# A two-layer transformer on one core: the same instructions in another planned order, from a plan that prices the tensor engine's changes of array mode and the delays between engines differently

## The chip, the core and the metric

The kernel runs on one core of a Trainium2 chip. Its engines work side by side, each through its own list of instructions: TensorE (PE, with its weight loads as PEld), VectorE (DVE), ScalarE (ACT), GpSimd (POOL), and SyncE (SP), which issues the transfers. They wait for each other by semaphores only. The metric is the time of one execution on the device, in microseconds (us).

## The reference, cut to what matters

Eight sequences of 1024 tokens of width 256 go through two layers, all in float32. Each layer is attention and then a feed-forward part, each added to its input:

```
x = x + attn0(layernorm(x))      # 16 heads of 16, causal, softmax
x = x + ffn0(layernorm(x))       # gates by entmax15 over 16 experts, GELU
x = x + attn1(layernorm(x))      # 16 heads of 16 from a latent of 64, half of each head rotated by position
x = x + ffn1(layernorm(x))       # shared squared-ReLU block; routed experts count only where a gate is exactly 1
```

## The kernel before, in words

A sequence is cut in two halves of 512 queries (`c` is 0 or 1). A pass is one half of one layer of one sequence; the half with `c` = 1 sees 1024 keys, the other 512. A pass has four units, each of four heads (`u`, 0 to 127). What one unit does:

- `ld`: its stacks of K and Q (float16 pieces of the float32 numbers) are loaded from DRAM, four transfers on SP.
- `s` (line 1282, masks on line 1296): TensorE makes scores by query, two banks at a time, and VectorE takes the largest of each row (lines 1877, with the causal mask, and 1880).
- `mx`, `mt`: GpSimd splits the maxima, TensorE turns them (line 1307), ScalarE copies them (line 1625), two transfers put them beside Q.
- `st` (line 1321): TensorE makes the scores again, transposed and with the maximum taken off, two banks at a time; ScalarE takes the exponential (line 1616), GpSimd clears what lies above the diagonal (line 1777).
- `pv` (line 1340): TensorE weighs the values; ScalarE copies the sum out (`o`, line 1631), and transfers and a division follow (`os`, `ol`, `rc`, `rs`, `rl`, `dv`).

Beside the units run the chains of the other work: layer norms (`rstd`, `norm`, `xt`), projections (`qk_`, `qk`, line 1251, `v_`, `v`, line 1259), the output product (`ao_`, `ao`), the feed-forward parts (`lg` to `fo`, with the GELU products `hid` on line 1395 and `z` on line 1400; `rt` to `down`). Every result of TensorE takes one of seven banks of the accumulation memory, which comes free when VectorE or ScalarE has read it.

What sets the order: before the kernel is built, `program_order()` (from line 603) plays the run through in a small model, `Plan`, and writes down one list, ORDER. Each engine then walks this list and issues its own part of it, so the model fixes the order on all engines and which bank each product takes; on the chip only semaphores decide when something starts. In the model a product takes its entry of TIMES (or a formula), a change of the array's mode costs SWITCH (`run`, from line 304; MODES says which products use the whole array, `full`, and which only 64 rows, `rows`, or strips of 32 columns, `strips`), a result is seen by the next engine SEEN later, and where several things could be next, that with the lowest rank is taken. The ranks are a row of RULES, one for each window of the program (27 windows, each with up to two passes and the chains that run beside them): `s` and `st` for a score step, `fed` and `fed_st` for the same while the engine that reads them has more than `feed_dve` or `feed_act` us of work, `pair` for two `pv` in a row, `due` and `chain` for the other products, `stay` the penalty for leaving the array's mode.

The line of `projection` that the change edits orders the first steps too: wmax is the largest weight by which the first layer's Q and K weights are scaled, `wm`, `sca` (line 1233), `scb` (line 1238).

## Time and profile before

| | |
|---|---|
| median of 3 runs | 2695.77 us (2695.38 to 2698.12) |
| the profiled execution | 2700.38 us, its span 2698.4 us |
| granted TensorE clock, mean over the span | 0.964 of 2.4 GHz |
| busy PE, DVE, ACT, POOL | 2440.8, 2042.8, 1869.6, 1031.5 us |
| instructions | 53735 |

The span is the time from the first to the last instruction of the program. TensorE is busy for 90% of it, but a matmul counts as busy while it waits inside the array too, so this is no proof that the array works at its peak.

### The profile page before, as it was taken

How to read it: one execution, taken by the hardware profiler on the slowest of the kernel's cores; microseconds unless marked ns; L12 is line 12 of the kernel's file. 1: busy time of each engine (PE TensorE's matmuls, PEld its weight loads, DVE VectorE, ACT ScalarE, POOL GpSimd, SP SyncE). 2: the span in 40 equal slices, each digit the busy share in tenths (PEclk: the TensorE clock that was granted, in tenths of full speed). 3: DMA queues.
4: the chain of work that ended last, by engine and by line, in shares of the span. 5: the costliest groups of instructions: out<-in, count | busy, mean ns of one | idle time of the engine just before them, and what ended most of it. 6: DMA issues, size and time to landing. Idle time of an engine off the chain costs nothing. (4 is left out here: it accounts for less than half of the span.)

```text
span 2698.4 us, 53735 instructions
## 1 busy us (share of the span) xinstructions
PE 2440.8 (90%) x17565; PEld 976.1 (36%) x17565; DVE 2042.8 (76%) x5616; ACT 1869.6 (69%) x3804; POOL 1031.5 (38%) x1710
## 2 busy tenths in 40 slices
PE   6889789999899998999999999999999999989785
PEld 3324233334333343333433343333433334334223
DVE  4884787967879578885888779786897868784862
ACT  3577467777677766687677777677677777856572
POOL 2324443254424363153532545244452534343221
PEclk9899899999899999999999999999999999989897
DMA  5311222224212242222421133212331222211211
GB/s 189 93 46 48 88 68 87 69 74 120 93 60 81 65 124 81 64 74 73 121 82 60 64 100 116 66 61 75 117 107 55 86 84 86 76 57 45 78 56 65
DMA packets 192482, 219.47 MB, mean 81 GB/s; under 512 B 36912, under 2 KB 143824, under 8 KB 192208
## 3 DMA queue, kind: packets, MB, share of 16 engines
q1 hardware_dynamic: 192208, 215.97, 26.1%
q8 instruction: 153, 2.51, 0.4%
q14 instruction: 121, 0.99, 0.1%
HBM read 113.07 MB, written 101.71 MB: 80 GB/s over the span
## 5 line engine op out<-in xcount | busy, mean ns | idle before, releaser
L1616 ACT ACTIVATE probs<-ps 128x512 f32<-128x512 f32 (+2 forms) x2560 | 1245.7, 560 | 465.8 <-PE ps L1321 458.6
L1880 DVE TENSOR_REDUCE mx<-ps 128x1 f32<-128x512 f32 (+2 forms) x1536 | 897.4, 638 | 233.4 <-PE ps L1282 134.0
L1877 DVE CUSTOM_DVE_ANT_0 ps<-ps,mask_b 128x512 f32<-128x512 f32 (+1 forms) x1024 | 613.7, 651 | 188.3 <-PE ps L1282 179.2
L1777 POOL TENSOR_SCALAR_AFFINE_SELECT probs<-probs 128x256 f32<-128x256 f32 (+1 forms) x768 | 368.9, 484 | 930.9 <-ACT probs L1616 927.1
L1340 PE MATMUL ps<-probs,vaug 128*17 128x512 f32 (+3 forms) x6144 | 602.3, 501 | 14.8 <-ACT probs L1616 6.1
L1282 PE MATMUL ps<-stk_k,stk_q 48*128 48x512 f16 (+3 forms) x3072 | 460.9, 336 | 87.5 <-issue 29.0
L1321 PE MATMUL ps<-stk_q,stk_k 50*128 50x512 f16 (+3 forms) x3072 | 451.5, 333 | 70.2 <-DVE mx L1877 23.1
L1321 PEld LDWEIGHTS ps<-stk_q,stk_k 50*128 50x128 f16 x3072 | 139.7, 94 | 465.8 <-issue 334.4
L1282 PEld LDWEIGHTS ps<-stk_k,stk_q 48*128 48x128 f16 x3072 | 141.7, 95 | 455.0 <-issue 322.1
L1251 PE MATMUL ps<-turned,wqkv 128*128 128x512 f32 x512 | 278.6, 640 | 8.9 <-ACT turned L1555 3.8
L1340 PEld LDWEIGHTS ps<-probs,vaug 128*17 128x17 f32 x6144 | 139.5, 97 | 293.6 <-issue 208.0
L1767 POOL TENSOR_TENSOR parts<-scratch,parts 128x512 f16<-128x512 f32 x128 | 148.2, 1158 | 108.9 <-ACT scratch L1581 86.5
L1568 ACT ACTIVATE xn<-x,shift,rstd 128x256 f32<-128x256 f32 x256 | 139.4, 603 | 44.1 <-POOL shift L1753 44.1
L1259 PE MATMUL ps<-wo,yT 128*128 128x256 f32 x512 | 145.1, 413 | 14.2 <-issue 8.6
L1877 DVE DVE_READ_ACCUMULATOR2_ANT mx<- 128x1 f32 x1024 | 144.6, 141 | 0.0
L1400 PE MATMUL ps<-ffn,win 128*128 128x512 f32 x256 | 143.1, 641 | 0.0
L1259 PE MATMUL ps<-wqkv,turned 128*128 128x256 f32 x512 | 138.1, 400 | 1.5 <-ACT probs L1616 0.8
L1894 DVE TENSOR_TENSOR x<-ps,x 128x512 f32<-128x512 f32 x128 | 87.8, 687 | 61.4 <-PE ps L1259 60.4
L1797 POOL TENSOR_SCALAR low<-mx 128x16 f32<-128x16 f32 x128 | 34.5, 269 | 257.1 <-DVE mx L1885 187.4
L1806 POOL TENSOR_TENSOR yT<-yT,inverse 128x512 f32<-128x512 f32 x64 | 81.4, 1272 | 115.1 <-DMA inverse<-inverse_sums 114.9
L1625 ACT ACTIVATE mT<-ps 8x512 f16<-8x512 f16 x128 | 73.8, 577 | 66.8 <-PE ps L1307 66.3
L1395 PE MATMUL ps<-ffn,wout1T 128*128 128x512 f32 x256 | 116.7, 608 | 2.0 <-DVE ffn L1971 1.8
(165 smaller groups left out, 2543.9 us busy)
## 6 DMA issues: line engine op xcount, KB each, us to landing
o<-oT SPq DMA_DIRECT2D x128, 256.0 KB, 2.2
stk_q<-q SPq DMA_DIRECT2D x256, 96.0 KB, 2.5
stk_k<-k SPq DMA_DIRECT2D x128, 192.0 KB, 3.6
q<-parts SPq DMA_DIRECT2D x64, 256.0 KB, 2.1
k<-parts SPq DMA_DIRECT2D x64, 256.0 KB, 2.1
yT<-o SPq DMA_DIRECT2D x64, 256.0 KB
inverse<-inverse_sums SPq DMA_DIRECT2D x64, 256.0 KB
stk_k<-k SPq DMA_DIRECT2D x128, 96.0 KB, 2.4
```

What stands on the lines that cost most here:

```text
L1251: ins = pe.matmul(pt, wqkv[l][:, kd, D * w + P * m:D * w + P * (m + 1)], xT(2 * l, b, c, kd), start=kd == 0, stop=kd == KD - 1)
L1259: ins = pe.matmul(pt[:, D * i:D * (i + 1)], left(kd)[:, cols], right(kd), start=kd == 0, stop=kd == n_k - 1)
L1282: ins = pe.matmul(out[:, width * a:width * (a + 1)], q, stk_k[rows, slot, h + a, BANK * p:BANK * p + width], start=a == 0, stop=a == n - 1 ...
L1321: ins = pe.matmul(out[:, width * k:width * (k + 1)], stk_k[rows, slot, h + k, P * j:P * (j + 1)], stk_q[rows, slot, h + k, cols], start=Tr ...
L1340: ins = pe.matmul(o_bank[32 * h:32 * h + DH + 1, cols], vaug[:, v, j % TPC, HG * g + h, :], probs[:, STEP[u, j] % PBUF, h, cols], start=j ...
L1400: ins = pe.matmul(acc, win2[:, k, :], hsb[k], start=k == 0, stop=k == OC - 1)
L1568: ins = act.activation(xn[:, t, :], src[:, t, :], ACT.Identity, bias=shift[:, i, t:t + 1], scale=rstd[:, i, t:t + 1])
L1616: act.activation(probs[:, step % PBUF, heads, cols], src, ACT.Exp, scale=exponent[l])\
L1767: pool.tensor_tensor(parts[:, o % PRING, 1], qf[o % QRING], parts[:, o % PRING, 0], ALU.subtract)\
L1777: pool.affine_select(out=diag, in_=diag, compare_op=ALU.is_ge, fill=0.0, base=0, pattern=[[0, k], [1, P]], channel_multiplier=-1).then_inc ...
L1877: dve.tensor_tensor_reduce(tile, tile, mask_b[:, BANK - width:BANK], 1.0, LOWEST, ALU.add, ALU.max, most)\
L1880: dve.tensor_reduce(most, tile.rearrange("q (k w) -> q k w", k=k), AX.X, ALU.max)\
```

## The change

The instructions stay as they are, and their number; only their order changes, and with it which bank each product takes. In the plan's model: entering the whole array's mode costs 0.1 us more (LOADED, which `run` adds to SWITCH), a result is seen 0.1 us after its engine is done instead of 0.06 (SEEN), and a `pv` costs 0.02 us less. A score step is not planned before VectorE's planned work is down to `ahead_dve`, an `st` not before ScalarE's is down to `ahead_act` (3.2 to 5 us and 2.3 to 5 us). The ranks of nearly all windows are other numbers. `projection` for the first layer now begins only after the statistics of its tokens. The buffer of the statistics has three parts instead of two, so that a layer norm of the second attention doesn't share one with that of the last feed-forward part.

```diff
 def projection(b, l, c):
-    steps = normalisation(2 * l, b, c) + ([] if b else [("after", ("scb", l))])
+    steps = ([] if l else [("after", ("stat", b, c))]) + normalisation(2 * l, b, c) + ([] if b else [("after", ("scb", l))])
...
-SEEN = 0.06
+SEEN = 0.1
...
+LOADED = {"full": 0.1}
...
-        self.pe = self.ran = max(self.pe, start) + time + (SWITCH if mode != self.mode else 0.0)
+        self.pe = self.ran = max(self.pe, start) + time + (SWITCH + LOADED.get(mode, 0.0) if mode != self.mode else 0.0)
...
-        self.run("pv", start, 4 * (z - a) / 2400 + 0.03)
+        self.run("pv", start, 4 * (z - a) / 2400 + 0.01)
...
-Rule = namedtuple("Rule", "feed_dve feed_act fed fed_st st s late due pair chain stay pace lead spread")
+Rule = namedtuple("Rule", "feed_dve feed_act fed fed_st st s late due pair chain stay pace lead spread ahead_dve ahead_act")
...
-    (1.89, 0.83, 2, 2.42, 5.63, 6.96, 3.84, 7.04, 5.16, 5, 2.1, 0.59, 2, 0.93),
+    (0.75, 0.6, 2, 3.4, 7.77, 7.73, 4, 7.04, 6.39, 5, 2.54, 1.08, 2, 0.58, 4.75, 5),
...
         if time is not None:
+            time = max(time, plan.busy["DVE"] - rule.ahead_dve)
...
             if time is not None:
+                time = max(time, plan.busy["ACT"] - rule.ahead_act)
...
-        st6 = sb("st6", [P, 2, TPC, 6])
+        st6 = sb("st6", [P, 3, TPC, 6])
...
-                six = st6[:, 1 if n else 0]
+                six = st6[:, (n + 1) // 2]
```

Two places on TensorE show what the new order is. In these rows stands the line, the operation, the tile written and those read, and the size; the lines after the change are 3 higher. The first place is the start of TensorE's list. Before:

```order
L1226 MATMUL ps<-ident,xn 128x128 x8
L1233 MATMUL ps<-ident,wmax 2x128
L1238 MATMUL ps<-wdiag,ones 128x4
L1251 MATMUL ps<-turned,wqkv 128x512 x8
L1259 MATMUL ps<-wqkv,turned 128x256 x8
```

Now, at the same place of TensorE's list:

```order
L1236 MATMUL ps<-ident,wmax 2x128
L1241 MATMUL ps<-wdiag,ones 128x4
L1229 MATMUL ps<-ident,xn 128x128 x8
L1254 MATMUL ps<-turned,wqkv 128x512 x8
L1262 MATMUL ps<-wqkv,turned 128x256 x8
```

The two small products of the weights' scale have moved ahead of the turning of the first normed tokens.

The second place is on TensorE near the end, where the last `pv` of unit 119 (17x256 and 17x128) are followed by scores of units 120 and 121 (`ps<-stk_k,stk_q`) until the first transposed scores of unit 120 (`ps<-stk_q,stk_k`). Before:

```order
L1340 MATMUL ps<-probs,vaug 17x256 x4
L1340 MATMUL ps<-probs,vaug 17x128 x4
L1282 MATMUL ps<-stk_k,stk_q 128x384 x2
L1282 MATMUL ps<-stk_k,stk_q 128x512 x4
L1282 MATMUL ps<-stk_k,stk_q 128x256 x4
L1296 MATMUL ps<-mask_b,ident_b 128x2x128 x2
L1296 MATMUL ps<-mask_x,ident_x 128x2x128 x2
L1282 MATMUL ps<-stk_k,stk_q 128x512 x4
L1282 MATMUL ps<-stk_k,stk_q 128x128 x4
L1296 MATMUL ps<-mask_b,ident_b 128x256 x2
L1296 MATMUL ps<-mask_x,ident_x 128x256 x2
L1282 MATMUL ps<-stk_k,stk_q 128x512 x10
```

Now, from the same `pv` of unit 119 on, up to the transposed scores of unit 120:

```order
L1343 MATMUL ps<-probs,vaug 17x256 x4
L1343 MATMUL ps<-probs,vaug 17x128 x4
L1285 MATMUL ps<-stk_k,stk_q 128x512 x4
L1310 MATMUL ps<-ident_h,mparts 8x128 x4
L1285 MATMUL ps<-stk_k,stk_q 128x512 x2
L1285 MATMUL ps<-stk_k,stk_q 128x384 x4
L1285 MATMUL ps<-stk_k,stk_q 128x512 x2
L1324 MATMUL ps<-stk_q,stk_k 128x512 x4
```

Before, 16 score steps stood in a row here with nothing between them but one turning of maxima; now there are 6. The other ten stand further ahead, between the `pv` and the transposed scores of unit 119.

## Rows read from the trace of the kernel before

**Rows 1.** The page, part 1: busy us, share of the span, instructions.
```profile
PE 2440.8 (90%) x17565; PEld 976.1 (36%) x17565; DVE 2042.8 (76%) x5616; ACT 1869.6 (69%) x3804; POOL 1031.5 (38%) x1710
```

**Rows 2.** Stretches: us, busy us (count) of each engine, granted clock, DMA share, GB/s.
```profile
60.00:2600.00 2540.00, 2342.91 (x16937) 923.88 (x16928) 1985.54 (x5461) 1802.92 (x3667) 991.57 (x1638) 0.97 0.26 79
200.00:300.00 100.00, 80.18 (x529) 33.57 (x529) 57.55 (x172) 57.47 (x117) 44.94 (x68) 0.90 0.21 68
2500.00:2600.00 100.00, 81.59 (x633) 27.63 (x633) 83.80 (x212) 60.01 (x126) 20.56 (x45) 0.86 0.23 64
2509.50:2527.50 18.00, 9.98 (x64) 2.99 (x57) 18.00 (x43) 1.18 (x2) 0.69 (x3) 0.61 0.39 91
```

**Rows 3.** Groups by line, whole span: busy us, mean ns | idle before, by releaser.
```profile
L1616 ACT ACTIVATE probs<-ps 128x512 f32<-128x512 f32 (+2 forms) x2560 | 1245.7, 560 | 465.8 <-PE ps L1321 458.6 <-issue 0.6
L1880 DVE TENSOR_REDUCE mx<-ps 128x1 f32<-128x512 f32 (+2 forms) x1536 | 897.4, 638 | 233.4 <-PE ps L1282 134.0 <-PE ps L1296 93.9 <-POOL mparts L1799 0.9
L1877 DVE CUSTOM_DVE_ANT_0 ps<-ps,mask_b 128x512 f32<-128x512 f32 (+1 forms) x1024 | 613.7, 651 | 188.3 <-PE ps L1282 179.2 <-POOL mparts L1799 5.2 <-DVE hr L2000 0.7
L1340 PE MATMUL ps<-probs,vaug 128*17 128x512 f32 (+3 forms) x6144 | 602.3, 501 | 14.8 <-ACT probs L1616 6.1 <-ACT oT L1631 4.8 <-POOL probs L1777 2.5
L1282 PE MATMUL ps<-stk_k,stk_q 48*128 48x512 f16 (+3 forms) x3072 | 460.9, 336 | 87.5 <-issue 29.0 <-DMA stk_k<-k 15.7 <-DVE mx L1880 15.6
L1321 PE MATMUL ps<-stk_q,stk_k 50*128 50x512 f16 (+3 forms) x3072 | 451.5, 333 | 70.2 <-DVE mx L1877 23.1 <-ACT probs L1616 20.2 <-DVE mx L1880 15.3
L1877 DVE DVE_READ_ACCUMULATOR2_ANT mx<- 128x1 f32 x1024 | 144.6, 141 | 0.0
```

**Rows 4.** Timeline of the start: start us, us, engine, line [idle before <-releaser].
```profile
10.27 1.27 DVE L2041 TENSOR_REDUCE wmax<-wqkv 128x1 f32<-128x512 f32 x2
14.01 1.94 PE L1226 MATMUL ps<-ident,xn 128*128 128x128 f32 x8 [14.01 <-ACT xn L1568]
15.87 0.37 PE L1233 MATMUL ps<-ident,wmax 128*2 128x128 f32 x1
15.98 0.60 ACT L1555 ACTIVATE turned<-ps 128x512 f32<-128x512 f32 x1 [0.26 <-PE ps L1226]
19.52 9.89 PE L1251 MATMUL ps<-turned,wqkv 128*128 128x512 f32 x16 [1.23 <-DVE unscale L2064]
34.21 1.15 PE L1226 MATMUL ps<-ident,xn 128*128 128x128 f32 x8 [1.34 <-ACT vaug L1598]
```

**Rows 5.** Timeline of PE where it hardly waits, at the full clock.
```profile
2438.62 7.03 PE L1395 MATMUL ps<-ffn,wout1T 128*128 128x512 f32 x16
2445.49 1.02 PE L1400 MATMUL ps<-ffn,win 128*128 128x512 f32 x2
...
2555.72 1.05 PE L1340 MATMUL ps<-probs,vaug 128*17 128x512 f32 x8
2556.71 0.39 PE L1321 MATMUL ps<-stk_q,stk_k 50*128 50x512 f16 x2
2556.93 0.60 PE L1282 MATMUL ps<-stk_k,stk_q 48*128 48x512 f16 x4
...
2561.91 0.38 PE L1282 MATMUL ps<-stk_k,stk_q 48*128 48x512 f16 x2
2562.22 1.13 PE L1387 MATMUL ps<-turned,ws 128*128 128x512 f32 x2
2563.28 0.39 PE L1321 MATMUL ps<-stk_q,stk_k 50*128 50x512 f16 x2
```

**Rows 6.** Timeline of PE: two of its long waits for transfers.
```profile
284.10 1.36 PE L1282 MATMUL ps<-stk_k,stk_q 48*128 48x512 f16 x6 [11.44 <-DMA stk_k<-k]
...
702.69 1.17 PE L1321 MATMUL ps<-stk_q,stk_k 50*128 50x512 f16 x4 [3.36 <-DMA stk_q<-mT]
```

**Rows 7.** Timeline of PE at the end.
```profile
2648.97 1.00 PE L1340 MATMUL ps<-probs,vaug 128*17 128x256 f32 x16 [1.03 <-POOL probs L1777]
...
2665.85 5.94 PE L1259 MATMUL ps<-wo,yT 128*128 128x256 f32 x16 [6.55 <-issue]
```

52 rows, old and new, of the table RULES are left out of this document.

## The prediction

> **What bounds the kernel now.** I read the page's busy shares first, then the idle time before each group of instructions, then the stretches, then the timeline where these pointed. TensorE is busy for 2440.8 of 2698.4 us and idle for 257.6; no other engine comes near over the whole span [rows 1]. So the end is set by TensorE: by the work in its list, and by its waits. The waits are for banks to be read. Before the scores it waits 87.5 us and before the transposed scores 70.2 us, largely on VectorE's maxima and ScalarE's exponentials, while these same engines wait 233.4 + 188.3 us and 465.8 us for TensorE [rows 3]. Each side waits for the other at different times: the mean load would allow less, only its distribution doesn't. The plainest case is near the end: for 18 us VectorE is busy for all 18.00, ScalarE for 1.18, TensorE for 9.98, at a granted clock of 0.61, so most of it at 1.2 GHz [rows 2]. Sixteen score steps stand in a row there, each of which fills two banks in 0.22 us, and VectorE needs 1.2 us to read them. What a new order can win is of this kind. What it can't win: the start, where TensorE has nothing before 14.01 us [rows 4], and the end, where a chain of transfers holds it for 6.55 us [rows 7]. The last rows of the list, from the last `pv` of unit 127 on, are nearly the same in both orders, so the roughly 50 us from 2648.97 to the end stay.
>
> **The start.** Scaling the weights waits on wmax, ready at 10.27 + 1.27 = 11.54 us, but its product comes at 15.87, behind the turning of the tokens; from there it takes 19.52 - 15.87 = 3.65 us until the projection may start. The turned tokens are there after the second of two 0.60 us copies, at 16.6 us [rows 4]. With the product first, the weights are ready at about 11.8 + 3.65 = 15.5 us, the tokens are late next, and the projection starts at about 16.7 instead of 19.52: 2.8 us less. VectorE's filling of constants, which follows the scaling, comes as much earlier, and with it the copy for which TensorE waits 1.34 us before 34.21 [rows 4]. Bounds: 0, if a transfer is late next, and 4, with that wait gone too. I take 2.8.
>
> **Changes of the array's mode.** Where nothing waits, eight `hid` take 7.03 us, less the last one's overlap 6.87, so 0.86 each in a row of whole-array products; one alone between two scores takes 2563.28 - 2562.22 = 1.06, and the score ahead of it 0.31 instead of 0.22 (2556.93 - 2556.71 is the plain one): 0.29 us for going there and back. A `pv` alone takes 2556.71 - 2555.72 = 0.99 against 0.86 in a row: with the 0.09 before it, 0.22 us [rows 5]. Counted in the two orders, the changes of mode go from 2426 to 2396: runs of strips from 547 to 520, of whole-array products from 726 to 729, the rest is changes between these two. At 0.11 us a change, and 0.07 more for each whole-array run, that is 30 x 0.11 - 3 x 0.07 = 3.1 us less. So the term for which the plan was given LOADED hardly moves: as many entries as before. Bounds 2 to 4.5 us.
>
> The rows show 0.07 us more for a visit to the whole array than for one to the strips. The Trainium skill (TensorEngine Tiling (Array Packing), Key Properties) says that changing the tiling mode drains the engine, and knows one price for all changes: at one price of 0.145 us the sum would be 4.4 us less, still small.
>
> **The balance between engines.** This is the main term, and it has no row of its own, so I work it from the order and the busy times. Each step is charged to its engines by the rows: a maximum 897.4/1536 = 0.58 us or, with the mask, (613.7 + 144.6)/1024 = 0.74 us, two of them a step; an exponential 1245.7/2560 = 0.49 us on average, by its width [rows 3]. I cut both orders into stretches of 12 us of TensorE's clean work and added up by how much VectorE's or ScalarE's work in a stretch exceeds 12 us (mean over where the cuts fall). Before, that is 198 us, after the change 182. With stretches of 6 us it is 280 and 264, with 25 us 130 and 119: 11 to 16 us less at every grain. In the trace before, the real time of such stretches exceeds TensorE's clean work by 1.0 us for each us of VectorE's excess and by 0.2 for ScalarE's, with a correlation of 0.8; put on the new order this gives 14 us less (11 to 16 over grains of 6 to 35 us). The largest part lies where the 16 score steps become 6. There each step costs 1.2 us against 0.22 of TensorE's own work; 10 steps moved out are worth at most 10 x 1.0 us, and they must be read by VectorE beside unit 119, where it has room but not for all. Score steps beyond the third in a row go from 22 to 9 in the whole order. Bounds: 0, if VectorE's work is only moved to where it is as late, and 30, if the two grow better in step than stretches can show. I take 14.
>
> **Tight pairs.** In the new order fewer products stand right behind what they wait for: a unit's first `pv` less than 1.5 us of work after the last of the unit before, 24 times before, 14 now; a projection less than 1.5 us after the turning, 14 and 9 of 32. All waits before `pv` are 14.8 us, of them 4.8 for the copy of the sum [rows 3]. I take 2 us less, between 0 and 6.
>
> **The other edits** (a third statistics buffer, `projection` behind its statistics, two more limits in the plan) add no instruction, and no engine waits longer for them: the statistics are ready on VectorE before GpSimd's root in both orders. The order of the long wait at 284 us is kept as well: the loads for unit 12 come behind the last rotated K, with 10.5 us of TensorE work between projection and score before and 10.6 now, so the 11.44 us stay [rows 6], and so does the stretch at clock 0.90 around it [rows 2].
>
> **Sum.** 2.8 + 3.1 + 14 + 2 = 22 us less, from the profiled execution 2700.4 - 22 = 2678. That execution is 4.6 us above the median of the runs shown, so 2674 there. As the 14 is a fit and each new order brings some waits of its own (next part), I keep 20: **2676 us**, its own range 2662 to 2689.
>
> **Rivals.**
> Drained banks bound it, whatever the order (no change). For it: VectorE's and ScalarE's maxima and exponentials are the same work in both; the excess falls by only 8% (198 to 182), and five of seventeen parts of the program have more of it than before, by 2 to 4 us each. Against: both engines wait for TensorE hundreds of us [rows 3]. It would leave the start and the modes, less about as much lost elsewhere: 2693 us. The Trainium skill warns of just this (TensorEngine Tiling (Array Packing), PSUM Bottleneck: a faster TensorE leaves the copies out of PSUM as the bound). The trace agrees for the 18 us stretch [rows 2], not for the whole.
>
> Long waits at new places (slower). A wait of the kind before 284.10 costs 11.44 us, and behind it the array runs at half clock, 0.90 over that 100 us [rows 6, 2], which is 20 us at 1.2 GHz and so up to 10 us more: about 20 us in all. The nearest candidates are the second layer's pass from unit 120 on, whose Q and K chain has 18.6 us of TensorE work before its first score instead of 20.3, and the first layer's from unit 108, 14.6 instead of 22.2. In the trace the rotated chain needed 10.5 + 11.4 = 22 us at unit 12, so at unit 120 3 or 4 us of wait with its clock loss is possible. The plain chain stood 13.1 us before unit 16 and no wait above 1.2 us came of it, which speaks against unit 108. The gain is gone from one such 20 us wait on; two of them make 2696 + 18 = 2714 us.
>
> The clock multiplies the gain (much faster). 0.036 of the clock is missing over the span, which is 97% of full speed even in the middle [rows 2]; fewer bursts would leave fewer falls. If the waits before scores, 87.5 + 70.2 us [rows 3], shrank by a quarter, 39 us, the time would be 2655 us. Against: the excess shrinks by 8%, not by 25%.
>
> The Trainium skill (TensorE: Matmul & The Clock Gate, HAM oscillation) says that idle gaps make the array's clock fall, and that this is paid again each time. By that rule alone each long wait removed gives more than its length. The trace agrees at 2509.5 us, where the granted clock is 0.61 [rows 2].
>
> **Chances.** Forecast 0.60, no change 0.17, slower 0.12, much faster 0.11. A measurement of this kernel can tell about 0.2%, 5.4 us. Faster by more than that (below 2690.4) holds the forecast, the last rival and a little less of rounding: 0.72; within it 0.16; slower 0.12. The range reaches up to 2700 for most of the no-change case and down to 2656 for part of the fast one.
>
> **What would show it.** Right: TensorE's projection starts at about 16.7 us; the stretch that holds the score steps of units 120 and 121 has TensorE busy well above 10 of 18 us; idle before lines 1282 and 1321 (1285 and 1324 now) falls together from 158 to about 140 us; busy VectorE and ScalarE are the same within 1%; unit 12's first score still waits about 11 us; the end from the last `pv` on lasts about 50 us. Wrong: a new wait above 5 us for a stack load, a mean clock below 0.964, or idle time that only moved from VectorE's banks to ScalarE's.

## The result, and the profile after

The change makes the kernel faster by half a percent: 2683.17 us median (2676.44 to 2687.72, 6 runs) against 2695.84 (2693.05 to 2700.16, 6 runs), a ratio of 0.9949 with a 95% interval of 0.9935 to 0.9963. That is about 14 us, where 20 were forecast. The profiled execution took 2683.06 us with a span of 2681.1; before it was 2700.38 and 2698.4.

The first view is the page after, part 1: busy us, share of the span and instructions of each engine. It answers to [rows 1].

```profile
PE 2444.6 (91%) x17565; PEld 973.5 (36%) x17565; DVE 2039.9 (76%) x5616; ACT 1869.1 (70%) x3804; POOL 1032.1 (38%) x1710
```

TensorE's idle time went from 2698.4 - 2440.8 = 257.6 us to 2681.1 - 2444.6 = 236.5, so 21.1 us less. But its busy time went up by 3.8 us, with the same matmuls and fewer changes of mode. The next view says where. It is a set of stretches (us, length, busy us and count of each engine, granted clock, DMA share, GB/s) of the kernel after: the middle, three that answer to [rows 2], and the stretches of list entries 554 to 3090 and 3565 to 6099. The two lists hold the same set of entries up to each of the entries 554, 3090, 3565 and 6099, so these two stretches do the same work in both kernels; the 18 us from 2509.50 don't, for the new order is some 14 us further on there. The row from 2496.80 to 2519.90 runs from the first `pv` of unit 119 to the first transposed scores of unit 120.

```profile
60.00:2600.00 2540.00, 2359.22 (x17019) 924.97 (x17017) 1990.46 (x5484) 1811.71 (x3687) 995.13 (x1647) 0.96 0.26 79
200.00:300.00 100.00, 79.11 (x500) 34.38 (x499) 54.91 (x161) 58.31 (x117) 45.12 (x66) 0.88 0.20 64
2509.50:2527.50 18.00, 13.92 (x92) 3.53 (x84) 15.78 (x36) 6.92 (x14) 1.83 (x5) 0.72 0.25 65
2496.80:2519.90 23.10, 17.02 (x142) 4.88 (x140) 20.32 (x48) 10.33 (x22) 3.81 (x10) 0.92 0.24 69
...
292.40:1327.60 1035.20, 986.38 (x7086) 393.22 (x7086) 823.08 (x2274) 757.25 (x1540) 426.62 (x701) 0.97 0.27 84
1530.50:2598.20 1067.70, 991.62 (x7172) 385.68 (x7170) 831.14 (x2266) 758.52 (x1547) 416.25 (x685) 0.97 0.26 79
```

The same two stretches in the kernel before, in the same columns:

```profile
299.40:1350.50 1051.10, 981.57 (x7087) 392.17 (x7086) 825.94 (x2263) 759.07 (x1542) 426.35 (x701) 0.98 0.27 83
1549.20:2612.20 1063.00, 987.93 (x7175) 387.78 (x7171) 826.71 (x2264) 757.70 (x1548) 415.82 (x683) 0.97 0.26 79
```

In the first half the same work takes 15.9 us less, in the second 4.7 us more. In both TensorE is busy for some 4 to 5 us more than before, and in the first its granted clock is lower (0.97 against 0.98). "The clock" below compares this with the other executions of the same two orders. Over the span the clock went from 0.964 to 0.959, and the time at the lower of its two levels (1.2 GHz) from 194 to 222 us, summed from the trace's clock records. The whole span, cut at five places up to which the two lists hold the same entries, from the two profiles (us):

| entries | before | after | difference | at half clock, before and after |
|---|---|---|---|---|
| to 314 | 183.9 | 175.6 | -8.3 | 34, 27 |
| 314 to 554 | 115.6 | 116.8 | +1.2 | 21, 27 |
| 554 to 3090 | 1051.1 | 1035.2 | -15.9 | 34, 55 |
| 3090 to 3565 | 198.6 | 202.9 | +4.3 | 7, 10 |
| 3565 to 6099 | 1063.0 | 1067.7 | +4.7 | 61, 72 |
| 6099 to the end | 86.2 | 82.9 | -3.3 | 35, 28 |

The groups by line of the kernel after (busy us, mean ns | idle before, by releaser), which answer to [rows 3]:

```profile
L1619 ACT ACTIVATE probs<-ps 128x512 f32<-128x512 f32 (+2 forms) x2560 | 1246.4, 559 | 451.2 <-PE ps L1324 444.1 <-issue 0.2
L1343 PE MATMUL ps<-probs,vaug 128*17 128x512 f32 (+3 forms) x6144 | 612.7, 511 | 7.2 <-POOL probs L1780 4.0 <-ACT oT L1634 1.2 <-ACT probs L1619 0.9
L1285 PE MATMUL ps<-stk_k,stk_q 48*128 48x512 f16 (+3 forms) x3072 | 463.2, 337 | 79.5 <-issue 23.5 <-DMA stk_k<-k 21.4 <-DVE mx L1883 12.6
L1324 PE MATMUL ps<-stk_q,stk_k 50*128 50x512 f16 (+3 forms) x3072 | 453.6, 336 | 72.3 <-DVE mx L1880 22.2 <-DVE mx L1883 22.0 <-ACT probs L1619 17.7
```

The idle time before scores fell by 8.0 us, before `pv` by 7.6, and before the transposed scores it rose by 2.1. The start and the end, on TensorE's timeline (start us, us, engine, line, operation, names, shapes, count [idle before <- releaser]); they answer to [rows 4, 6 and 7]:

```profile
11.86 0.37 PE L1236 MATMUL ps<-ident,wmax 128*2 128x128 f32 x1 [11.86 <-DVE wmax L2044]
...
17.05 9.10 PE L1254 MATMUL ps<-turned,wqkv 128*128 128x512 f32 x16 [0.88 <-ACT turned L1558]
...
276.92 1.04 PE L1285 MATMUL ps<-stk_k,stk_q 48*128 48x512 f16 x4 [12.82 <-DMA stk_k<-k]
...
2648.95 5.57 PE L1262 MATMUL ps<-wo,yT 128*128 128x256 f32 x16 [6.51 <-issue]
```

The projection starts at 17.05 instead of 19.52, behind the turned tokens, as foreseen. The wait at unit 12 is still there, and so is the one at the end.

### The profile page after: what moved, and what is told of

It is laid out like the page before. It is cut to its first block, busy times and chain, and to the rows that moved or that the text cites. A ratio compares the mean times of both kernels' runs of the same rounds, so it can differ in the third digit from the quotient of the medians.

```text
span 2681.1 us, 53736 instructions
## 1 busy us (share of the span) xinstructions
PE 2444.6 (91%) x17565; PEld 973.5 (36%) x17565; DVE 2039.9 (76%) x5616; ACT 1869.1 (70%) x3804; POOL 1032.1 (38%) x1710
## 3 DMA queue, kind: packets, MB, share of 16 engines
q1 hardware_dynamic: 192208, 215.97, 26.1%
## 4 chain that ended last, share of the span: by engine, by line
PE 65%; DVE 21%; ACT 4%; issue 3%; DMA 3%; POOL 1%; SPq 1%; DVEq 0%; ACTq 0%; POOLq 0%
PE ps L1343 15%; PE ps L1262 9%; PE ps L1285 9%; PE ps L1324 8%; PE ps L1254 8%; DVE mx L1883 7%; PE ps L1403 5%; DVE ps L1880 5%; PE ps L1398 4%; ACT probs L1619 3%; PE ps L1390 2%; PE ps L1229 2%; PE ps L1299 2%; DMA sums<-o 1%; DVE st L1847 1%
## 5 line engine op out<-in xcount | busy, mean ns | idle before, releaser
L1343 PE MATMUL ps<-probs,vaug 128*17 128x512 f32 (+3 forms) x6144 | 612.7, 511 | 7.2 <-POOL probs L1780 4.0
L1770 POOL TENSOR_TENSOR parts<-scratch,parts 128x512 f16<-128x512 f32 x128 | 148.3, 1160 | 77.2 <-ACT scratch L1584 63.8
L1754 POOL TENSOR_TENSOR rstd<-veps,neg_half 128x4 f32<-128x4 f32 x64 | 66.2, 1034 | 152.6 <-DVE veps L1856 152.6
```

The source lines that it names most:

```text
L1343: ins = pe.matmul(o_bank[32 * h:32 * h + DH + 1, cols], vaug[:, v, j % TPC, HG * g + h, :], probs[:, STEP[u, j] % PBUF, h, cols], start=j ...
L1770: pool.tensor_tensor(parts[:, o % PRING, 1], qf[o % QRING], parts[:, o % PRING, 0], ALU.subtract)\
```

## The experiments

Each kernel holds both planners and builds its list from them; the diffs show the lines that choose. Ratios are to the kernel before, on the same chip, with their 95% intervals.

### Which part of the list brings the gain

Since the two lists agree as sets at some places, either list can be followed up to one of them and the other from there on, with each bank as its own plan has it. Four such splices (0 is the list of before, 1 that of after):

```diff
-ORDER = program_order()
+ORDER, TAKEN = spliced([(1, 314), (0, 6216)])
+ORDER, TAKEN = spliced([(0, 554), (1, 3090), (0, 6216)])
+ORDER, TAKEN = spliced([(0, 3565), (1, 6099), (0, 6216)])
+ORDER, TAKEN = spliced([(1, 3090), (0, 6099), (1, 6216)])
```

**The start alone.** 

> The first 314 entries of the list in the new order, the other 5902 in the old one (both orders have done the same set of entries at that point; the new kernel's third statistics buffer is kept). In the two traces the new order is 8.3 us ahead at entry 314, 4.0 of it at the setup. Theory A (differences belong to their place in the list and add up): 8 us less than before, about 2688. Theory B (a lead won early is used up later, since VectorE's bursts or a transfer are late next): within 3 us of before, and the lead of the trace shrinks along the list. Predicted for the start alone were 2.8 us, for everything before entry 314 nothing was said.

**Entries 554 to 3090 alone.** 

> Only entries 554 to 3090 in the new order, the rest in the old one. This stretch takes 1051.1 us before and 1035.2 after the change in the two traces. Theory A: 16 us less than before, about 2680, nearly the whole gain of the change from two fifths of the list. Theory B (the two traces differ there by chance of one execution, or the lead goes again): 0 to 8 us less.

**Entries 3565 to 6099 alone.** 

> Only entries 3565 to 6099 in the new order: the stretch in which the 16 score steps in a row become 6, for which the prediction had the largest single gain. In the traces it takes 1063.0 us before and 1067.7 after. Theory A: 5 us more than before, about 2700: the prediction named the wrong place. The prediction's own view: 5 to 10 us less. Theory B: about the same as before.

**The start, the first half and the end.** 

> The new order up to entry 3090, the old one from there to entry 6099, the new one for the end. Theory A: the sum of the traces' differences, 22.9 to entry 3090 and 3.3 at the end, so 26 us less than before, about 2670, and 9 to 13 us less than the new order. Theory B: no better than the new order, 2680 to 2690.

Measured, with before at 2703.11 us; each time each kernel moved the way its theory A says, and the first half and the second moved by more than the two profiles differ:

| | median us | ratio | interval |
|---|---|---|---|
| the start | 2691.16 | 0.9961 | 0.9945 to 0.9977 |
| the first half | 2679.89 | 0.9909 | 0.9889 to 0.9930 |
| the second half | 2714.59 | 1.0046 | 1.0029 to 1.0064 |
| start, first half, end | 2670.58 | 0.9886 | 0.9864 to 0.9908 |

The second half of the new order is a loss, and the place to which the prediction gave "the largest part" of its main term lies in it. The first half alone gains more than the whole change. The differences about add up: 0.9961 x 0.9909 = 0.9870 against 0.9886 for both with entries 314 to 554 and the end. The fourth kernel is the best of this case, about 31 us under before. From it to the change (0.9949) only entries 3090 to 6099 differ: 17 us, of which the second half has 12; the 4.3 us of entries 3090 to 3565 in the two profiles would be the rest, but no kernel has them alone. In its profile too the same work takes less in the first half and no more in the second (entries 554 to 3090 and 3565 to 6099):

```profile
292.50:1331.80 1039.30, 989.50 (x7088) 394.00 (x7088) 823.51 (x2277) 758.55 (x1541) 428.05 (x701) 0.97 0.28 84
1531.30:2586.00 1054.70, 982.42 (x7178) 386.05 (x7175) 825.82 (x2264) 757.62 (x1548) 417.01 (x683) 0.98 0.27 80
```

### The row of 16 score steps by itself

```diff
-ORDER = program_order()
+MOVES = [
+    (("s", 120, 7, 1, 1), ("s", 120, 7, 0, 1)), (("s", 120, 6, 0, 0), ("st", 119, 5, 0)), (("s", 120, 6, 1, 0), ("s", 120, 6, 0, 0)),
...
+    (("s", 121, 7, 1, 0), ("os", 119)), (("mx", 120), ("s", 121, 7, 1, 0)),
+]
+ORDER, TAKEN = moved(*spliced([(0, 6216)]), MOVES)
```

`moved` puts the first entry of each pair right behind the second. Of the 16 steps, 12 stand in the list shown ahead; the other four follow behind the turning of the maxima, with which that list ends.

> The order before with one edit at the place where the prediction put the largest part of the gain: ten score steps of units 120 and 121 go from the row of 16 into the transposed scores and pv of unit 119, as the change has them; all else and every bank stays. Theory A (the prediction's step: 10 steps moved out are worth up to 10 x 1.0 us, since VectorE reads them beside unit 119): 5 to 10 us faster than before, ratio 0.996 to 0.998, and the time from st 118 4 0 to st 121 0 0 falls from 76.8 us by as much. Theory B (VectorE's maxima bound the whole region from unit 119 on, so the wait only moves from the row of 16 to the steps ahead of it; with after, the lag of TensorE behind its clean work grows by 25.4 us from unit 117 to 121 where before has 27.2): 0 to 2 us faster, ratio 0.999 to 1.001.

Measured: 2705.83 us, ratio 1.0019 (1.0005 to 1.0032): no gain, rather 5 us more. The same entries in the kernel before, from `st` 119 4 0 to `st` 120 0 0 (a stretch's row: us, length, busy us and count by engine, clock, DMA share, GB/s):

```profile
2501.50:2527.50 26.00, 16.68 (x120) 4.86 (x117) 24.44 (x57) 7.61 (x17) 4.66 (x10) 0.73 0.44 108
```

and with the ten steps moved:

```profile
2505.50:2533.50 28.00, 16.57 (x120) 5.15 (x117) 24.73 (x57) 8.06 (x17) 4.71 (x10) 0.77 0.38 100
```

VectorE is busy for 24.4 of the 26 us before the move. The 8 us ahead of the row, into which the steps went, leave it only 1.6 us of room. The stretch that the expectation names, from `st` 118 4 0 to `st` 121 0 0, took 80.9 us where before has 76.8. The timeline of TensorE with the steps moved shows the waits at their new places:

```profile
2510.10 0.39 PE L1401 MATMUL ps<-stk_k,stk_q 48*128 48x512 f16 x2 [0.60 <-DVE mx L1996]
2511.44 0.39 PE L1401 MATMUL ps<-stk_k,stk_q 48*128 48x512 f16 x2 [0.95 <-issue]
2512.54 0.34 PE L1440 MATMUL ps<-stk_q,stk_k 50*128 50x384 f16 x2 [0.71 <-DVE mx L1999]
```

The transposed scores (L1440) and `pv` now queue behind score steps that wait for VectorE, so ScalarE's work is held up too.

But this kernel does not place the steps as the change does, though its expectation says so: `moved` left the first score steps of unit 120 where they stood, at `st` 119 4 0. In the new list they begin right behind `st` 119 0 1. The room is there, just ahead, on VectorE's timeline before:

```profile
2502.21 2.48 DVE L1880 TENSOR_REDUCE mx<-ps 128x1 f32<-128x512 f32 x4 [11.62 <-PE ps L1282]
```

TensorE could not use it in the old order, for the stack of unit 120 landed at 2501.0 us, and its first score started at 2501.7. In the kernel after, the last projection for unit 120 starts 13.8 us ahead of unit 119's first transposed scores instead of 6.0, the stack lands at 2490.8, and the first score starts at 2491.0. From the first transposed scores of unit 119 to those of unit 120, before and then after:

```profile
2491.30:2527.50 36.20, 23.82 (x179) 6.85 (x179) 24.44 (x57) 16.64 (x34) 13.93 (x18) 0.81 0.48 122
```

```profile
2489.90:2519.90 30.00, 23.27 (x180) 6.45 (x176) 24.64 (x56) 15.89 (x32) 9.48 (x15) 0.84 0.40 105
```

With nearly the same busy time on TensorE and VectorE this place takes 6.2 us less after the change, and 4.2 less in the kernel with the second half alone. The earlier projection seems to be paid for just ahead: over units 117 to 121 together, TensorE's lag behind its clean work (the time that has passed, less the undisturbed times of its products) grows by 25.4 us after and 27.2 before, so 2 us are left of it.

### The long waits of the second half

After the change, entries 3565 to 6099 hold ten waits above 1 us that sum to 20.2 us, where before has eight with 11.8; with this stretch alone eight of the ten are there again at the same entries, and all its waits above 1 us sum to 23.4 us. One of them in the kernel after, on TensorE's timeline and then on VectorE's:

```profile
1755.37 0.61 PE L1324 MATMUL ps<-stk_q,stk_k 50*128 50x512 f16 x2 [2.82 <-DVE mx L1883]
```

```profile
1754.42 0.35 DVE L1892 RECIPROCAL sums<-sums 128x32 f32<-128x32 f32 x1 [4.26 <-DMA sums<-o]
1754.69 1.22 DVE L1883 TENSOR_REDUCE mx<-ps 128x1 f32<-128x512 f32 x2
```

VectorE stands for 4.26 us at a reciprocal whose sums are still on their way; the maxima queued behind it could have freed banks, and TensorE waits for these. The next kernel moves such entries, and nothing on TensorE:

```diff
-ORDER = program_order()
+MOVES = [
+    (("rl", 101), ("ld", 106)),
+    (("rc", 83), ("s", 86, 7, 1, 1)), (("rs", 83), ("st", 84, 4, 0)), (("rl", 83), ("pv", 84, 3)), (("dv", 83), ("rstd", 2, 5, 0)),
+    (("stat", 7, 0), ("s", 99, 6, 0, 0)), (("rstd", 0, 7, 0), ("s", 99, 6, 1, 0)),
...
+    (("add", 7, 1, 1, 1, 0), ("st", 118, 7, 0)), (("add", 7, 1, 1, 1, 1), ("add", 7, 1, 1, 1, 0)),
+]
+ORDER, TAKEN = moved(*spliced([(1, 6216)]), MOVES)
```

> The order after the change, with nothing moved on TensorE and every bank as it was; only other queues are changed, at four places of the second half: on SyncE the load of unit 106's stack goes ahead of a load that stands behind unit 101's store (TensorE waits there 3.5 us in the profile after); on VectorE the division of unit 83's sums goes behind two score steps (2.8 us before st 84 3 1) and the statistics of the pass 7 0 behind three (3.2 us before st 97 5 0); on GpSimd two additions go behind the masks of st 118 (2.4 us before pv 118 5). Theory A (the second half lost because entries that wait for a transfer stand ahead of bank reads in an in-order queue, and each such wait also lowers the granted clock): 3.5 + 2.8 + 3.2 + 2.4 = 12 us of waits go, less some 3 us that come elsewhere, and some 3 us of half clock come back: 12 us less than after, ratio to before 0.990 to 0.992 where after has 0.9949. Theory B (those waits are only where the lag of VectorE and ScalarE becomes visible; taken away they come back at the next steps): the time of after within 3 us, ratio 0.994 to 0.996.

Measured: 2692.53 us, ratio 0.9956 (0.9941 to 0.9972), where after has 0.9949. Theory B holds. All four waits are gone, but each has a successor, and the stretch again has ten waits above 1 us, now 22.7 us in sum. For the first one, the timelines of TensorE and of GpSimd:

```profile
1766.77 1.62 PE L1381 MATMUL ps<-wo,yT 128*128 128x256 f32 x3 [5.16 <-POOL yT L1928]
```

```profile
1765.41 1.26 POOL L1928 TENSOR_TENSOR yT<-yT,inverse 128x512 f32<-128x512 f32 x1 [4.21 <-DMA inverse<-inverse_sums]
```

The reciprocal came later, so its transfers came later, and the product that needs the division waits 5.16 us where the maxima had waited 2.82. For the statistics 2.0 us before `pv` 97 5 came in place of 3.2. Instead of 3.49 us for the stack of unit 106 there are 3.95 before the transposed scores behind it (1.5 there after the change), and instead of 2.4 before `pv` 118 5 there are 3.14 for the stack of unit 120, on TensorE's timeline:

```profile
2158.56 0.61 PE L1443 MATMUL ps<-stk_q,stk_k 50*128 50x512 f16 x2 [3.95 <-DVE mx L1999]
...
2498.43 0.61 PE L1404 MATMUL ps<-stk_k,stk_q 48*128 48x512 f16 x2 [3.14 <-DMA stk_k<-k]
```

The best splice was mended in the same way at two places of its first half:

```diff
+MOVES = [
+    (("stat", 4, 0), ("s", 50, 6, 1, 1)),
+    (("at", 0, 1), ("s", 12, 2, 1, 0)), (("g", 0, 1, 0), ("at", 0, 1)), (("g", 0, 1, 1), ("g", 0, 1, 0)),
+]
+ORDER, TAKEN = moved(*spliced([(1, 3090), (0, 6099), (1, 6216)]), MOVES)
```

> The best splice so far (new order up to entry 3090, the old one to 6099, the new end; 2670.6 us, ratio 0.9886), with two places mended: the statistics of the pass 4 0 go behind two score steps (they wait 4.3 us for the load of x, and TensorE waits 4.2 us before st 49 0 0), and the gate product at 0 1 goes behind the score steps s 12 2, for it waits 4.2 us for the gates while the scores' stack is already there. Theory A (the waits go): 4 + 2.4 = 6 us less, some 2 us of half clock back: ratio 0.985 to 0.987. Theory B (they come back at the next steps): ratio 0.988 to 0.989.

Measured: 2675.14 us, ratio 0.9897 (0.9878 to 0.9916), no better than 0.9886. Here too the waits only moved. The one before `st` 49 0 0 shrank from 4.2 to 1.0 us, but the next score step, `s` 50 5 1 0, now waits 4.21 us, and the stretch that holds both took 1038.2 instead of 1039.3 us. The gate product's wait of 4.2 us became one of 6.07 and one of 1.65:

```profile
284.48 0.50 PE L1397 MATMUL ps<-stk_k,stk_q 48*128 48x384 f16 x2 [6.07 <-issue]
286.62 1.05 PE L1488 MATMUL ps<-ident,cum 128*48 128x128 f32 x4 [1.65 <-DVE mx L1992]
...
1032.90 1.09 PE L1397 MATMUL ps<-stk_k,stk_q 48*128 48x512 f16 x6 [4.21 <-issue]
```

### What a microsecond of TensorE's work is worth

```diff
+def parted(order):
+    """(pv, a score step) for every pair of pv of a unit that a score step follows, and then no pv."""
...
+        if a[0] == b[0] == "pv" and a[1] == b[1] and x[0] == "s" and y[0] != "pv" and ("o", b[1]) not in order[pe[k + 1]:pe[k + 2]]:
+            moves.append((b, x))
...
+ORDER, TAKEN = (lambda o, t: moved(o, t, parted(o)))(*spliced([(0, 6216)]))
```

> The order before, with 75 pairs of pv parted: where pv a, pv b of one unit are followed by a score step, pv b goes behind that step. The runs of strips go from 547 to 622, the changes of mode from 2393 to 2540; instructions, banks and all else stay. Theory A (each visit to the strips costs 0.22 us, as the rows of the clean stretch say, and TensorE sets the end nearly everywhere): 75 x 0.22 = 16.5 us more, ratio 1.006. Theory B (at most of these places TensorE waits for a bank soon after, so the price vanishes in that wait): 0 to 6 us more, ratio 1.000 to 1.002. Between them the ratio gives the share of a TensorE price that reaches the end. The score step begins about 0.5 us earlier and pv b 0.25 us later, which should be worth less than 3 us either way.

Measured: 2708.41 us, ratio 1.0017 (1.0002 to 1.0032), so 4.6 us (0.5 to 8.6) for 75 visits, 0.06 us each where the clean rows say 0.22. The profiled execution has TensorE 29 us busier (2470.0) and idle for 2718.3 - 2470.0 = 248.3 us, 9.3 less than before [rows 1]. That execution was 12 us above its kernel's median, so of the 29 us a part is slow clock; the median is the better witness. About a quarter of a TensorE price reached the end, and the interval allows 3 to 52%; what the score steps win by starting earlier (under 3 us by the expectation) is not taken out of this.

The price itself is there. From the first `pv` of a pair to what follows the three entries, the 75 places together take 17.7 us more in this trace than in that of before, with a median of 0.22. So it is the rest of the run that gives most of it back, and not soon after, as theory B has it: in the trace of before only 26 of the 75 places have an idle gap above 0.1 us on TensorE within 6 us, none within 2 us.

```profile
PE 2470.0 (91%) x17565; PEld 967.7 (36%) x17565; DVE 2043.9 (75%) x5616; ACT 1868.8 (69%) x3804; POOL 1031.7 (38%) x1710
```

### Costs, ranks and limits of the plan

Leaving the two new limits out of the rules gives the new list again, entry for entry and bank for bank. They do nothing here. On the ranks, the kernel's description ahead has one thing the wrong way round: the condition in the code is `plan.busy['DVE'] - now < rule.feed_dve`, so `fed` and `fed_st` hold while the engine that reads has less than `feed_dve` or `feed_act` us of work, not more. Costs and ranks were parted by two kernels:

```diff
+    kept, RULES = RULES, OLD_RULES
...
+    NEW, SEEN, LOADED = False, 0.06, {}
```

The first line makes the kernel with new costs and old ranks, the second the one with old costs and new ranks (NEW stands for the edits of `projection` and of the cost of `pv`). The single costs, SEEN, LOADED, the cost of `pv` and `projection`, were not parted from each other.

> The plan with the change's new costs (SEEN 0.1, LOADED 0.1, pv 0.02 less, projection behind its statistics, third statistics buffer) but the old table of ranks and no new limits: what the costs do alone. The planner then makes 686 whole-array runs where before has 705 and after 711, 2351 changes where before has 2393; TensorE's clean work falls by 5 us; but the work of VectorE and ScalarE that exceeds 12 us in stretches of 12 us of TensorE's work rises by some 30 us (from 255 to 285 in a count with full step costs; after has 213). Theory A (the distribution between the engines sets the time, the model's costs only change it through the ranks that were found with them): 30 x 0.9 - 5 = 22 us slower than before, ratio 1.005 to 1.011. Theory B (the costs bring the gain, fewer and better placed changes of mode): 5 to 14 us faster than before, ratio 0.995 to 0.998.

> The plan with the change's new table of ranks but the costs of before (SEEN 0.06, no LOADED, pv 0.03, projection as before). Its order has 655 whole-array runs and 2331 changes of mode, fewer than before (705, 2393) and after (711, 2368), clean work 7 us under before; the excess of VectorE and ScalarE over 12 us stretches is 307 us where before has 255, after 213 and the old ranks with the new costs 285. Theory A (the distribution between the engines sets the time; either table of ranks is good only with the costs it was found with): from the kernel with old ranks and new costs, 39 us slower at 30 more of excess, this one with 52 more comes out 40 to 65 us slower than before, ratio 1.015 to 1.024. Theory B (the ranks bring the gain and the new costs cost something, or the other way round): the effects add up in ratios, 0.9949 / 1.0146 = 0.981, so about 50 us faster than before.

Measured: new costs alone 2741.75 us, ratio 1.0146 (1.0127 to 1.0165); new ranks alone 2789.34 us, ratio 1.0334 (1.0313 to 1.0355). Each half of the change makes the kernel slower, together they make it faster. Both have fewer changes of mode than before (2351 and 2331 against 2393) and less clean work, and both are slower, so theory B is out for both. Theory A has the direction, with both sizes guessed too small. Its count of excess work (213 us after, 255 before, 285 and 307 here) puts the four kernels in the order of their times; that the distribution is the cause is argued from this, not shown. The page of the second, part 1, with a span of 2783.0 us:

```profile
PE 2477.7 (89%) x17565; PEld 984.1 (35%) x17565; DVE 2035.6 (73%) x5616; ACT 1864.7 (67%) x3804; POOL 1030.6 (37%) x1710
```

TensorE is idle for 2783.0 - 2477.7 = 305.3 us there, 48 more than before [rows 1], and busy for 37 more, with 271 us at half clock instead of 194.

### Cuts where the lists don't agree

Two kernels tried to use the order's better parts more finely, with cuts where one to eight entries differ and the banks behind chosen anew:

```diff
+ORDER, TAKEN = banked(joined([(1, 3090), (0, 5691), (1, 6216)]), spliced([(1, 3090), (0, 6099), (1, 6216)]))
+ORDER, TAKEN = banked(joined([(1, 4404), (0, 5155), (1, 6216)]), spliced([(1, 6216)]))
```

> New order up to entry 3090, the old one to 5691 (about unit 116), then what is left in the new order's own sequence; at the second cut eight entries stand elsewhere than in either, and the banks behind it are chosen anew. The best splice so far (ratio 0.9886) with the new order for units 116 to 123 instead of the old one. Theory A (a gain or loss belongs to its place: in the two profiles TensorE's lag behind its clean work grows by 61.6 us from unit 115 to 123 before and by 47.3 after, so the new order's tail is 14 us better, though not at the row of 16 steps alone): 8 to 14 us faster than the best splice, ratio 0.9835 to 0.9855. Theory B (that lag only catches up a debt that the new order made between units 97 and 115, and the tail's own worth is nothing): ratio 0.988 to 0.990.

> New order up to entry 4404 (about unit 89), the old one to 5155 (about unit 104), then the new one again; three entries stand elsewhere at the first cut and a few at the second, and the banks behind the first cut are chosen anew. The change without the stretch in which it loses most: there the gain over before falls from 17.6 us at unit 95 to 4.9 at unit 103 in the two profiles, with waits of 3.2, 2.0, 3.5 and 1.5 us. Theory A (the loss belongs to that stretch): 8 to 13 us faster than after, ratio 0.990 to 0.992. Theory B (taken away here it comes back behind, as when the single waits were mended): ratio 0.994 to 0.996.

Measured: 2681.67 us, ratio 0.9940 (0.9921 to 0.9959), and 2709.44 us, ratio 1.0037 (1.0021 to 1.0053). Both expectations of a gain failed, and both kernels fell even outside what theory B gave. In the first, TensorE's lag behind its clean work grows by 43.6 us over units 116 to 119, where the uncut orders have 25.7 and 26.1; the displaced gate product alone waits 4.9 us. Whether the displaced entries or the new banks did it was not parted, so these two say only that a stretch's worth is not kept by a cut at which the lists differ.

## Why the prediction was right, and where it was not

**Right:** faster by 0.5%, inside the range, 7 us above the forecast; that the start gains; that the clean work and the modes hardly matter; that the waits between engines carry the gain; TensorE busy for more than 10 of 18 us around units 119 to 121 (17.02 of 23.10); the wait at unit 12 (12.82 us) and the end, from the last `pv` on about 48 us; VectorE's and ScalarE's busy times within 0.2%.

**Luck.** That the sum came so near is in part luck. The start and the first half of the list gave 10 and 25 us as the medians of their own kernels, the second half took 12 back and entries 3090 to 3565 perhaps 4. The prediction kept only 2 us for waits of the new order's own, and the gains that it summed, 22 us, are less than these 35.

**The start.** 2.8 us were given, 2.5 came at the projection and 4.0 at the first score step (63.8 to 59.8 us). By entry 314 it was 8.3, the additional 4.3 with 7 us less at half clock. The kernel with the new start alone gained 10 us (6 to 15). In the profiles the old list takes 183.0 to 185.6 us to entry 314 (before, and the kernels with the first and with the second half alone), the new one 174.9 to 177.3. So the term was mis-sized: 2.8 where 8 to 10 came. The clock has a part in it; what else lies between the first score step and entry 314 was not parted.

**Changes of mode.** 3.1 us were given at full price, for 30 changes fewer (2426 and 2396; 2393 and 2368 in the count that the expectations use). At the 0.06 us a visit of the parted pairs it is about 1 us or less. The price of 0.22 us holds where the change stands, as the parted pairs show; what it adds to the end is less, as waits elsewhere shrink. It isn't that changes stand just ahead of waits: in the trace before, 494 of the 2426 have an idle gap above 0.1 us on TensorE within 2 us.

**The balance and the tight pairs.** 14 and 2 us were given. Idle time fell by 21.1 us in all. Of this 7.6 stand before `pv` (14.8 to 7.2 us) and 8.0 - 2.1 = 5.9 before scores and transposed scores, where the main term was to show: the sign named for it, 158 to about 140 us, came at 151.8. Before `pv`, the wait for the copy of the sum, for which the tight pairs stand, fell from 4.8 to 1.2 us, and that for exponentials, which belongs to the balance, from 6.1 to 0.9. So the tight pairs gave nearer 4 than 2 us, and the balance shows before other products than those named.

The step of this term that failed is "The largest part lies where the 16 score steps become 6". The place does take 4 to 6 us less, but the scores of unit 120 start some 9 us earlier there against those of unit 119, which a projection moved ahead allows; over units 117 to 121, 2 us are left, and ten steps moved out of the row by themselves cost 5 us (1 to 9). The gain lies in entries 554 to 3090; where in them was not parted. Over units 115 to 123 TensorE's lag does grow by 14 us less than before (47.3 against 61.6), so the tail may be worth something after all: the kernel made to show it had entries displaced at its cut, so this stays open.

**The clock.** No term stood for it in the forecast, only a rival and a sign against the forecast ("a mean clock below 0.964"), and the sign came. TensorE's busy time should have fallen by 3.1 us by the prediction's count of clean work and rose by 3.8, with 28 us more at half clock. But one profile of each is a small sample. Here are the same two stretches in eight profiles (us; in brackets the time at half clock, and for the second stretch also the sum of TensorE's waits above 1 us):

| kernel | entries 554 to 3090 | entries 3565 to 6099 |
|---|---|---|
| before | old, 1051.1 (34) | old, 1063.0 (61; 11.8) |
| the start | old, 1054.5 (57) | old, 1053.8 (44; 8.6) |
| ten steps moved | old, 1055.1 (58) | old but for these, 1066.6 (58; 14.7) |
| the first half | new, 1038.3 (62) | old, 1061.0 (51; 12.6) |
| start, first half, end | new, 1039.3 (65) | old, 1054.7 (48; 7.0) |
| after | new, 1035.2 (55) | new, 1067.7 (72; 20.2) |
| the second half | old, 1056.1 (60) | new, 1071.0 (75; 23.4) |
| after, four places mended | new, 1034.3 (55) | new but for these, 1082.2 (99; 22.7) |

In the first stretch the old order has 57 to 60 us at half clock in three executions of four; the 34 of the profile before are the exception, so the lower clock there is not the new order's, and the gain of 12 to 22 us stands in every pair. In the second stretch the new order has 72 us and more at half clock and the old one 44 to 61. The mean granted clock over all executions of a kernel says the same: 0.962 to 0.964 for before (on each of four chips) and for every kernel with the old second half, 0.958 to 0.960 for after and the kernels with the new one. So the lower clock belongs to the second half of the new order. The Trainium skill (TensorE: Matmul & The Clock Gate, HAM oscillation) lets the clock fall after idle gaps. The traces agree in this stretch, where the longer sum of waits goes with more time at half clock; over the whole span they don't, for idle time fell while the time at half clock rose. The gaps of 0.2 to 1 us fell from 278 to 228, those above 2 us stayed 15 with 70.9 us instead of 68.8. Whether these waits are the cause is not shown.

**The rivals.** Long waits at new places did come, of 2 to 3.5 us instead of 11, and in the second half; they were priced near 20 us each, and the stretch that holds them lost 5 us in the profiled executions and 12 as the median of its own kernel. That a wait taken away gives its length back is refuted for the six that were: each came back soon after, as a wait for the same chain or for a bank. So they look like the places where a lag shows, not like its cause; what causes the lag of the second half stays open. Drained banks bound the 18 us in which VectorE is busy for 18.00, but not whatever the order: with the scores begun earlier, the place around them takes 6.2 us less. The Trainium skill's warning (TensorEngine Tiling (Array Packing), PSUM Bottleneck) holds for those 18 us, and the trace agrees there; over the whole span no engine but TensorE is above 76%.

## What to carry to other kernels

A row in which one engine starves another shows who is late there, not what moving work out of it will bring: look first at how busy the late engine is in the stretch into which the work would go, and, where it stands idle a little earlier, at what the work needs before it can start there (here a load, and so a projection). A price read where an engine doesn't wait was right at its place and about four times what reached the end. One profile of each kernel can mislead on the clock: further executions of the same stretch, in other kernels, told the exception from the rule. A planner's costs and the ranks found with them are one thing: the new costs alone made this kernel 1.5% slower, the new ranks alone 3.3% slower, both together 0.5% faster, and the best order was a splice of the two at places where both had done the same work.

## What the runs showed of the hardware that was not expected

The time at half clock differed between profiled executions by more than the orders explain: 192 us in the mended best splice, 210 in the best splice, 222 after, 250 in the mended after. Between the last two TensorE is idle for 236.5 and for 2695.1 - 2453.6 = 241.5 us, 5 us more, while busy time rose by 9 us with the same matmuls and the same order on TensorE.

```profile
PE 2453.6 (91%) x17565; PEld 975.7 (36%) x17565; DVE 2039.5 (76%) x5616; ACT 1870.3 (69%) x3804; POOL 1031.8 (38%) x1710
```

So 28 us more at half clock went with 9 us more of busy time and 14.0 us more of span (2681.1 to 2695.1); the 5 us of idle time can also come from the four moved places. A broader figure comes from the clock and time of every execution: among executions of one kernel on one chip (164 in 17 groups), each us more at half clock goes with 0.32 us more of the time, with a correlation of 0.8. This is an estimate from clocks that are given to 0.001. It is less than the half that a TensorE that is always the bound would show. By it, the lower clock of the kernel with the second half alone (0.9583, before 0.9632 on the same chip, so 27 us more at half clock) goes with about 8 of its 12 us. Which brings the other about, the waits the clock or the clock the waits, no run parts.
